# Attention and graph recurrence on one core: the adjacency product in 64x64 tiles, and an earlier start for chunk 0's graph attention

## Chip, core and metric

The kernel runs on one core of a Trainium2 chip. The metric is the device time of one execution in microseconds (us). TensorE (PE) multiplies matrices and transposes into PSUM, VectorE (DVE) and ScalarE (ACT) read PSUM and SBUF, GpSimd (POOL) works on SBUF and issues some DMAs, SyncE (SP) issues the others. They run side by side and meet at semaphores.

## What is computed

x is 128 batches of 64 nodes with 256 features. Four pre-norm residual layers follow each other; in each, `h = relu(layernorm(x))`:

```
x = x + attention_0(h)      # 8 heads, masked by adj, q k v o projections
x = x + attention_1(h)      # 8 heads, and a layernorm of its output added
x = x + graph_attention(h)  # hW; e = leaky(s1 + s2) * adj; softmax; elu(att hW + beta hW)
x = x + recurrence(h)       # 3 steps of:
    a  = adj @ h
    z  = sigmoid(w3(a) + u3(h));  r = sigmoid(w4(a) + u3(h))
    hv = tanh(w5(a) + u5(r * h)); h = (1 - z) * h + z * hv
```

adj (64x64) is symmetric and is the same for every batch, so that `in_mat` and `out_mat` of the recurrence are the same matrix and the two halves of w3, w4 and w5 are added beforehand.

## The kernel before

x stays in SBUF for the whole run as 64 tiles of 128 rows (two batches each), in 16 chunks of four tiles. Weight products are exact to fp32 by splitting both operands into a high and a low fp32r part, three matmuls for one (`product`, L99). PSUM is two tensors of four banks: `scores` (called `high` outside the attention) and `ring`.

**Attention.** `iterations` runs 32 iterations (T = 32, 16 chunks in each of two layers) as a pipeline: in iteration i PE multiplies the scores of chunk i (`scores_piece`), transposes the probabilities of chunk i-1 (`p_transposes`) and the rows of i+1, applies the output weights to i-2 (`o_products`), forms the values of i-1 (`values`), and projects q, k and v of i+1. The last loop body is i = T-2; everything of T-1 and later is written out by hand behind it on each engine, mixed with the graph attention of chunks 0 and 1. Each engine works strictly through its own list, so the order in which these calls are written is the order of the work.

**Graph attention** of one chunk goes: statistics (`rows_stats`, DVE), `norm` (POOL), `graph_normalise` (ACT), `graph_rows` (PE transposes), `graph_high` (ACT) and `graph_low` (DVE), four `graph_product` (PE) with `copy_hw` (ACT), `graph_s2` (PE), `graph_scores` (DVE), `g_shift` (POOL), `g_exponential` (ACT), `graph_attention` (DVE), `graph_attT` (PE), `copy_attT` (DVE), `graph_aggregate` (PE), `graph_out` (ACT and DVE). Then the same sort of norm (`recurrence_stats`, `norm(rn, ..)`, `norm_rows(rn, ..)`) and `enter` (PE, ACT, DVE) bring the chunk into the recurrence.

**Recurrence.** Two chunks run in turn, one step of one chunk is a "half", 48 of them, and a last one that only ends step 3. Six halves are a group of two chunks; from half 1 of each group on, the graph attention of the next two chunks is woven in (`graph_a`: transposes and products, `graph_b`: softmax and aggregation); the last group has none. PE's list in a half: transpose the new h to token rows (`tok`, in steps 2 and 3), u3 product, the adjacency product (L1545: eight matmuls of 128x128 by 128, since adjT is held block-diagonal for two batches), the u5 product of r*h, then w4, w3 and w5 products of the result `agg`. ACT's list: copy tok (L808), two tanh of z (L814), copy the first half of hu (L818), round r*h to its high part (L824, `rhp_hi`), copy the second half of hu (L829), copy agg's high parts (L835), tanh of hv (L839) and so on. DVE makes r*h (L1194), waits for `rhp_hi`, and forms the low part (L1196, `rhp_lo`), for which PE's u5 product waits.

## Time and profile before

| what | value |
|---|---|
| three runs, median (lowest to highest) | 1593.96 us (1591.88 to 1594.06) |
| the profiled execution, device time | 1595.16 us |
| its span in the trace | 1593.1 us |
| what lies around the span | 2.06 us |
| PE busy | 1510.5 us, 95% of the span |
| DVE, ACT, POOL busy | 1243.9, 993.0, 533.7 us |

How to read it: the times of steps below are starts in us from the span's start. The attention ends near 625 us, the recurrence runs from about 640 us to the end. Busy times are of one execution, and the device time is that of the span and 2.06 us around it.

### The profile page before, as it was taken

Reading aid. Unit: us, or ns where it says so; the run is one execution under the profiler, and the core shown is the slowest. Engines: PE = TensorE matmul, PEld = TensorE weight load, DVE = VectorE, ACT = ScalarE, POOL = GpSimd, SP = SyncE. Lnnn points to the kernel's source line nnn. Section 1 sums busy time; section 2 is a strip of 40 time slices with the busy share of each in tenths; the row PEclk is TensorE's granted clock in tenths of the full one; section 3 lists DMA queues with packets and bytes.
Section 4 is the critical chain, followed back from the end, with each engine's and each line's share of the span. In section 5 each row is a group of like instructions: output and inputs, shape, how many; then the busy total and the mean of one; then the engine's idle time right before and its main releaser. Section 6 shows DMA issues by size and latency. Waiting matters only on the chain.

```text
span 1593.1 us, 40455 instructions
## 1 busy us (share of the span) xinstructions
PE 1510.5 (95%) x16248; PEld 1299.4 (82%) x16248; DVE 1243.9 (78%) x2511; ACT 993.0 (62%) x1793; POOL 533.7 (34%) x622
## 2 busy tenths in 40 slices
PE   3899999899999987799999999999999999999997
PEld 3789989798888876588888888888888888888885
DVE  2787887988899986677877877877777777778666
ACT  3676677667777774565666566655665566566553
POOL 1666766667787893300101111111111111111000
PEclk9999999999999998899999999999999999999998
DMA  9200000003322242100000000000000000000000
GB/s 251 82 3 0 0 0 1 15 16 61 61 53 53 56 78 29 27 0 1 27 1 1 27 0 0 26 0 0 26 0 0 26 0 0 27 1 0 27 1 26
DMA packets 36760, 40.12 MB, mean 25 GB/s; under 512 B 11840, under 2 KB 31808, under 8 KB 36672
## 3 DMA queue, kind: packets, MB, share of 16 engines
q0 software_dynamic: 4608, 16.78, 5.6%
q1 hardware_dynamic: 32064, 22.10, 4.8%
q8 instruction: 64, 1.05, 0.3%
q14 instruction: 24, 0.20, 0.0%
HBM read 13.71 MB, written 8.39 MB: 14 GB/s over the span
## 4 chain that ended last, share of the span: by engine, by line
PE 68%; DVE 15%; ACT 7%; issue 5%; POOL 4%; DMA 1%; SPq 0%; DVEq 0%; POOLq 0%; ACTq 0%
PE ring L99 30%; PE scores L99 23%; PE scores L1545 3%; PE ring L1343 2%; PE scores L1307 2%; DVE rhp_lo L1196 2%; PE ring L1490 2%; DVE total L955 2%; POOL s L530 1%; PE ring L1380 1%; ACT rhp_hi L824 1%; ACT later_w L814 1%; PE ring L1508 1%; PE ring L1463 1%; ACT later_w L808 1%
## 5 line engine op out<-in xcount | busy, mean ns | idle before, releaser
L1196 DVE TENSOR_TENSOR rhp_lo<-r,rhp_hi 128x1024 fp32r<-128x1024 f32 x48 | 58.8, 1225 | 157.0 <-ACT rhp_hi L824 157.0
L530 POOL TENSOR_TENSOR s<-s,mx 128x512 f32<-128x512 f32 x128 | 137.9, 1102 | 46.3 <-DVE mx L951 46.3
L536 POOL TENSOR_TENSOR s<-s,rtotal 128x512 f32<-128x512 f32 x128 | 131.4, 1056 | 36.7 <-DVE rtotal L957 36.5
L594 POOL TENSOR_TENSOR r_var_eps<-r_mean_var,eps 128x4 f32<-128x4 f32 x16 | 8.1, 509 | 384.3 <-DVE r_mean_var L1105 384.3
L669 ACT ACTIVATE s<-s 128x512 f32<-128x512 f32 x128 | 78.4, 644 | 76.1 <-POOL s L530 75.9
L839 ACT ACTIVATE hv<-scores,bias 128x512 f32<-128x512 f32 x96 | 66.1, 689 | 83.6 <-PE scores L99 83.6
L946 DVE SCALAR_TENSOR_TENSOR s<-scores,mask 128x512 f32<-128x512 f32 x128 | 87.2, 681 | 32.4 <-PE scores L1307 32.4
L808 ACT ACTIVATE later_w<-ring 128x512 f32<-128x512 f32 x64 | 34.8, 595 | 121.9 <-PE ring L1508 121.9
L681 ACT ACTIVATE pT<-ring 128x512 f32<-128x512 f32 x128 | 66.1, 604 | 47.1 <-PE ring L1343 47.1
L951 DVE TENSOR_REDUCE mx<-s 128x8 f32<-128x512 f32 x128 | 87.9, 686 | 4.4
L857 ACT ACTIVATE r<-r,bias_half 128x512 f32<-128x512 f32 x96 | 64.3, 717 | 37.7 <-DVE r L1221 37.7
L99 PE MATMUL scores<-rhp_hi,u5T_hi 128*128 128x512 f32 x192 | 80.4, 419 | 4.0 <-DVE rhp_lo L1196 1.8
L955 DVE TENSOR_REDUCE total<-s 128x8 f32<-128x512 f32 x128 | 82.6, 645 | 0.0
L1232 DVE TENSOR_TENSOR later_w<-scores,hu 128x512 f32<-128x512 f32 x96 | 64.4, 686 | 19.6 <-PE scores L99 18.8
L99 PE MATMUL ring<-agg_hi,w4T_hi 128*128 128x512 f32 x192 | 78.9, 411 | 0.0
L99 PE MATMUL scores<-agg_hi,w3T_hi 128*128 128x512 f32 x192 | 78.3, 408 | 0.0
L594 POOL TENSOR_TENSOR g_var_eps<-g_mean_var,eps 128x4 f32<-128x4 f32 x16 | 7.3, 457 | 209.5 <-DVE g_mean_var L1105 209.5
L99 PE MATMUL scores<-agg_hi,w5T_hi 128*128 128x512 f32 x192 | 77.0, 401 | 0.0
L99 PE MATMUL ring<-agg_lo,w4T_hi 128*128 128x512 f32 x192 | 76.2, 397 | 0.0
L99 PE MATMUL ring<-agg_hi,w4T_lo 128*128 128x512 f32 x192 | 76.2, 397 | 0.0
L99 PE MATMUL scores<-agg_hi,w5T_lo 128*128 128x512 f32 x192 | 75.9, 395 | 0.0
L99 PE MATMUL scores<-rhp_lo,u5T_hi 128*128 128x512 f32 x192 | 75.8, 395 | 0.0
(295 smaller groups left out, 5251.2 us busy)
## 6 DMA issues: line engine op xcount, KB each, us to landing
x<-beta_less_one POOLq DMA_DIRECT2D x16, 512.0 KB, 4.6
x<-o POOLq DMA_DIRECT2D x16, 512.0 KB, 6.5
out_x<-x SPq DMA_DIRECT2D x16, 512.0 KB, 2.9
x<-in_x SPq DMA_DIRECT2D x1, 6656.0 KB, 30.5
later_w<-in_L_gnn_w_w SPq DMA_DIRECT2D x3, 512.0 KB, 7.2
x<-in_x SPq DMA_DIRECT2D x1, 1024.0 KB, 10.9
stage<-in_L_gnn_w_qkv SPq DMA_DIRECT2D x3, 256.0 KB, 3.0
x<-in_x SPq DMA_DIRECT2D x1, 512.0 KB, 3.5
```

What stands on the lines that cost most here:

```text
L99: last = pe.matmul(out, s, m, start=(begins and n == 0), stop=(ends and n == len(terms) - 1))
L530: pool.tensor_tensor(sr, sr, mx[:, r, :].unsqueeze(2).to_broadcast([P, CT * 2, N]), ALU.subtract).then_inc(s_shifted, 1)
L536: pool.tensor_tensor(sr, sr, rtotal[:, r, :].unsqueeze(2).to_broadcast([P, CT * 2, N]), ALU.mult).then_inc(p_ready, 1)
L669: act.activation(s[:, par, r, :, :, :], s[:, par, r, :, :, :], ACT.Exp).then_inc(p_exp, 1)
L681: act.activation(pT[:, r, :, :].rearrange("p t q -> p (t q)"), ring[:, r, :], ACT.Copy).then_inc(pT_copied, 1)
L839: act.activation(hv[:, m, :], high[:, 2 + m, :], ACT.Tanh, bias=bias[:, 2, m:m + 1])\
L857: act.activation(r[:, m, :], r[:, m, :], ACT.Tanh, bias=bias_half[:, 1, m:m + 1], scale=0.5)\
L946: dve.scalar_tensor_tensor(sr(par, r), scores[:, r, :].rearrange("p (a k) -> p a k", k=N), SCALE, masks[layer_of(i, lay)][:].unsqueeze(1). ...
L951: dve.reduce_max(mx[:, r, :], sr(par, r), AX.X).then_inc(s_max, 1)
L955: dve.reduce_sum(total[:, r, :], sr(par, r), AX.X).then_inc(p_total, 1)
L1196: dve.tensor_tensor(rhp.lo[:], r[:], f32(rhp.hi[:]), ALU.subtract).then_inc(rh_lo_ready, 1)
L1232: dve.tensor_tensor(z[:, m, :], high[:, m, :], hu[:, m, :], ALU.add).then_inc(z_added, 1)
```

## The change

Three things are changed.

1. **Adjacency product.** Instead of eight 128x128 matmuls with a block-diagonal matrix, 32 matmuls of 64x64 by 64: rows 0-63 and 64-127 (g), output partitions 0-63 and 64-127 (c), on four quarters of the array. What belongs to g goes to bank g, so each copy to `agg` writes a strided pattern, and both banks are ready only at the end.
2. **ACT's list in a half.** The rounding of r*h comes ahead of the two tanh of z and the first copy of hu.
3. **The seam between attention and recurrence.** The normalised rows, transposes and products of chunk 0's graph attention move into iteration T-2 (with `g_hT_first` as a buffer of its own), its softmax and output into the work of T-1. Chunk 1's transposed attention, aggregation, output and entry move behind the adjacency product of half 0. POOL's and ACT's output norms of the last attention chunks move too.

Two waits in a half on a loop's count are written with `wait_apart`. The core of the diff (renamed parameters, and DVE's hand-written list in part, are left out):

```diff
+        g_hT_first = Parts(plan, "g_hT_first", [P, FT, CW], start["later_w"] + 4096)
...
-        hw_next = sb("hw_next", [P, CT, WX], F32, start["s"] + 8192)
+        hw_next = sb("hw_next", [P, CT, WX], F32, start["w_ext"])
...
-        h = [sb(f"h_{q}", [P, FT, CW], F32, start["o_n"] + 4096 * n) for n, q in enumerate("ab")]
+        h = [sb("h_a", [P, FT, CW], F32, start["w1o_hi"]), sb("h_b", [P, FT, CW], F32, start["o_n"])]
...
+                norms(T - 1, 1, 1)
+                norm(gn, 1, 1)
                 pool.wait_ge(v_ready, T * 2)
+                pool.memset(att[:], 0.0).then_inc(att_cleared, 1)
                 pool.memset(adjT[:], 0.0).then_inc(adj_cleared, 1)
-                pool.memset(att[:], 0.0).then_inc(att_cleared, 1)
+                shift(T - 1, 1, 0)
+                shift(T - 1, 1, 1)
+                g_shift(0)
+                beta_to_x(T - 1, 1)
+                o_to_x(T - 1, 1, 1)
+                shift(T - 1, 1, 2)
+                shift(T - 1, 1, 3)
+                scale(T - 1, 1, 1)
+                for q in range(R):
+                    normalise(T - 1, 1, q)
+                norm(rn, 0, 0)
...
                 g_shift(1)
-                norm(rn, 0, 0)
                 norms(T + 1, 1, 1)
                 o_to_x(T + 1, 1, 1)
-                scale(T + 1, 1, 1)
-                norm(rn, 1, 1)
...
+                    if isinstance(i, int) and i == T - 2:
+                        graph_normalise(0, 0)
...
+                        if i == T - 2:
+                            graph_high(0, high, 0, g_hT_first)
...
+                        if isinstance(i, int) and i == T - 2:
+                            for t in range(CT):
+                                copy_hw(0, t, high, 2)
...
                     if not s.first:
+                        act.wait_ge(rh_done, n)
+                        if isinstance(n, int) and n == 1:
+                            act.wait_ge(x_plus_o, 16 * CHUNKS)
+                            act.wait_ge(x_plus_beta, 16 * CHUNKS)
+                        act.activation(rhp.hi[:], r[:], ACT.Copy).then_inc(rh_hi_ready, 1)
...
-                    if not s.first:
-                        act.wait_ge(rh_done, n)
-                        if isinstance(n, int) and n == 1:
-                            act.wait_ge(x_plus_o, 16 * CHUNKS)
-                            act.wait_ge(x_plus_beta, 16 * CHUNKS)
-                        act.activation(rhp.hi[:], r[:], ACT.Copy).then_inc(rh_hi_ready, 1)
...
+                        for g in range(2):
+                            act.wait_ge(agg_ready, n * FT + g + 1)
+                            act.activation(agg.hi[:].rearrange("p m (t g q) -> p g m t q", t=CT, g=2)[:, g],
+                                           high[:, g, :].rearrange("p (m t q) -> p m t q", m=FT, t=CT), ACT.Copy)\
+                                .then_inc(agg_hi_ready, 1)
...
+                    if s.first:
+                        o_normalise(T + 1, 1, 1)
...
+                    if s.first:
+                        graph_out(1, high, 2)
+                        norm_rows(rn, r_hn[1], 1, 1)
+                        enter(1, 1)
                     if s.graph_norm is not None:
                         graph_normalise(s.graph_norm, 0 if s.k == 0 else 1)
+                    if s.first:
+                        o_normalise(T + 2, 0, 1)
...
-                act.wait_ge(xT_ready, T * FT)
-                graph_normalise(0, 0)
                 copy_pT(T - 1)
                 o_normalise(T - 1, 1, 1)
-                for q in range(R - 1):
-                    exponential(T - 1, 1, q)
-                graph_high(0, high)
+                exponential(T - 1, 1, 0)
+                exponential(T - 1, 1, 1)
+                g_exponential(0)
+                graph_normalise(1, 1)
                 o_high(T - 2)
-                exponential(T - 1, 1, R - 1)
-                graph_normalise(1, 1)
+                exponential(T - 1, 1, 2)
+                exponential(T - 1, 1, 3)
+                graph_high(1, high, 2)
+                graph_out(0, high, 0)
+                copy_pT(T)
                 for t in range(CT):
-                    copy_hw(0, t, high, 2)
-                copy_pT(T)
-                graph_high(1, high)
+                    copy_hw(1, t, high, 2, hw_next)
+                norm_rows(rn, r_hn[0], 0, 0)
+                o_high(T - 1)
+                g_exponential(1)
+                enter(0, 0, high, 0)
                 o_normalise(T, 0, 1)
-                g_exponential(0)
-                o_high(T - 1)
-                for t in range(CT):
-                    copy_hw(1, t, high, 0, hw_next)
-                graph_out(0, high, 2)
-                g_exponential(1)
-                norm_rows(rn, r_hn[0], 0, 0)
-                graph_out(1, high, 0)
-                enter(0, 0, high)
-                o_normalise(T + 1, 1, 1)
                 act.wait_ge(b_ready, 5)
-                norm_rows(rn, r_hn[1], 1, 1)
...
+                    if isinstance(i, int) and i == T - 2:
+                        graph_low(0, high, 0, g_hT_first)
...
+                    if isinstance(i, int) and i == T - 2:
+                        rows_stats(gn, 1, x_final)
...
+                        for g in range(2):
+                            dve.wait_ge(agg_hi_ready, n * FT + g + 1)
+                            dve.tensor_tensor(agg.lo[:].rearrange("p m (t g q) -> p g m t q", t=CT, g=2)[:, g],
+                                              high[:, g, :].rearrange("p (m t q) -> p m t q", m=FT, t=CT),
+                                              f32(agg.hi[:]).rearrange("p m (t g q) -> p g m t q", t=CT, g=2)[:, g],
                                               ALU.subtract).then_inc(agg_lo_ready, 1)
+                    if s.first:
+                        copy_attT(1, high, 2)
...
+                    if s.first:
+                        graph_out(1, high, 2)
+                        recurrence_stats(1)
...
+                    if s.first:
+                        enter(1, 1)
...
-                sums(T - 1, 1, 0)
-                sums(T - 1, 1, 1)
-                graph_low(0, high)
-                sums(T - 1, 1, 2)
-                sums(T - 1, 1, 3)
+                graph_low(1, high, 2)
                 o_stats(T - 1, 1, 1)
-                final_sum(T - 1, 1, 1)
-                dve.tensor_scalar(beta_ident[:], ident[:], g_beta[:, 0:1], None, ALU.mult).then_inc(beta_ident_ready, 1)
-                graph_scores(0, high, 2)
-                graph_low(1, high)
                 take_first(T, 0, 1)
                 take_out(T - 2, 1, 0, 1)
...
-                graph_attention(1)
-                copy_attT(1, high, 0)
+                enter(0, 0, high, 0)
+                o_stats(T + 1, 1, 1)
                 final_sum(T, 0, 1)
...
+                    if isinstance(i, int) and i == T - 1:
+                        pe.wait_ge(g_hT_lo_ready, FT)
+                        pe.wait_ge(hw_copied, CT)
...
+                    if i == T - 2:
+                        pe.wait_ge(s_masked, (i + 1) * R)
+                        graph_rows(0, high)
...
+                        if isinstance(i, int) and i == T - 2:
+                            pe.wait_ge(g_hT_lo_ready, FT)
+                            pe.wait_ge(gw_lo_ready, 2)
+                            for t in range(CT):
+                                wait(pe, hw_copied, t - 1)
+                                graph_product(0, t, high, 2, g_hT_first)
...
-                            pe.wait_ge(tok_copied, (s.later - 1) * 2)
+                            wait_apart(pe, tok_copied, (s.later - 1) * 2)
...
-                            pe.wait_ge(z_added, n * FT)
+                            wait_apart(pe, z_added, n * FT)
...
-                            pe.wait_ge(x_plus_pos, 4)
...
                         rows = r_hn[s.me] if s.step == 0 else tok
-                        for m in range(FT):
-                            for t in range(CT):
-                                last = pe.matmul(high[:, m, t * P:(t + 1) * P], rows[:, t, m * P:(m + 1) * P],
-                                                 adjT[:], start=True, stop=True)
-                            last.then_inc(agg_ready, 1)
+                        for t in range(CT):
+                            for m in range(FT):
+                                for g in range(2):
+                                    own = slice(g * N, (g + 1) * N)
+                                    for c in range(2):
+                                        f = m * P + c * N
+                                        last = pe.matmul(
+                                            high[c * N:(c + 1) * N, g, (m * CT + t) * N:(m * CT + t + 1) * N],
+                                            rows[own, t, f:f + N], adjT[own, own], start=True, stop=True)
+                                    if t == CT - 1 and m == FT - 1:
+                                        last.then_inc(agg_ready, 1)
...
+                    if s.first:
+                        graph_attT(1, high, 2)
...
+                    if s.first:
+                        graph_aggregate(1, high, 2, hw_next)
...
+                        if s.first:
+                            pe.wait_ge(x_plus_pos, 4)
...
+                    if s.first:
+                        pe.wait_ge(hu_copied, FT)
+                        enter(1, 1)
...
                 scores_piece(T - 1)
                 p_transposes(T - 1, 1)
+                pe.wait_ge(s_masked, (T - 1) * R + 1)
+                graph_s2(0, high, 0, g_hT_first)
                 o_products(T - 1, 1)
-                pe.wait_ge(s_masked, (T - 1) * R + 2)
-                graph_rows(0, high)
                 values(T - 1, 1)
-                pe.wait_ge(g_hT_lo_ready, FT)
-                pe.wait_ge(gw_lo_ready, 2)
+                graph_attT(0, high, 0)
                 pe.wait_ge(s_masked, T * R)
-                for t in range(CT):
-                    wait(pe, hw_copied, t - 1)
-                    graph_product(0, t, high, 2)
-                graph_s2(0, high, 2)
+                graph_rows(1, high, 2)
+                graph_aggregate(0, high, 0)
                 p_transposes(T, 0)
-                graph_rows(1, high)
-                o_products(T, 1)
-                values(T, 0)
-                graph_attT(0, high, 2)
                 pe.wait_ge(g_hT_lo_ready, 2 * FT)
                 for t in range(CT):
                     if t >= 2:
                         pe.wait_ge(hw_copied, CT + t - 1)
-                    graph_product(1, t, high, 0)
-                graph_s2(1, high, 0)
-                graph_aggregate(0, high, 2)
+                    graph_product(1, t, high, 2)
+                o_products(T, 1)
+                graph_s2(1, high, 2)
+                values(T, 0)
                 o_products(T + 1, 1)
-                graph_attT(1, high, 0)
-                graph_aggregate(1, high, 0, hw_next)
                 pe.wait_ge(x_plus_pos, 2)
-                enter(0, 0, high)
+                enter(0, 0, high, 0)
                 halves(pe, half)
```

**PE, first loop group of the recurrence, half 1.** `hp` is h in its two parts, `g_hn` the normalised rows of the next chunk, `rhp` is r*h. Before:

```order
L99 MATMUL ring<-hp_b_lo,u3T_hi 128x512
L99 MATMUL ring<-hp_b_hi,u3T_lo 128x512
L1463 MATMUL ring<-ident,g_hn 128x128 x8
L1545 MATMUL scores<-adjT,r_hn_b 128x128 x8
L99 MATMUL scores<-rhp_hi,u5T_hi 128x512
L99 MATMUL scores<-rhp_lo,u5T_hi 128x512
```

and now:

```order
L99 MATMUL ring<-hp_b_lo,u3T_hi 128x512
L99 MATMUL ring<-hp_b_hi,u3T_lo 128x512
L1508 MATMUL ring<-ident,g_hn 128x128 x8
L1593 MATMUL scores<-adjT,r_hn_b 64x64 x32
L99 MATMUL scores<-rhp_hi,u5T_hi 128x512
L99 MATMUL scores<-rhp_lo,u5T_hi 128x512
```

Only the adjacency product has another form; its neighbours are the same.

**ACT, half 2 of the first group** (`later_w` is tok in the first row and z in the next, `e` the graph softmax). Before:

```order
L808 ACTIVATE later_w<-ring 128x512 x2
L814 ACTIVATE later_w<-later_w,bias_half 128x512 x2
L818 ACTIVATE hu<-ring 128x512
L824 ACTIVATE rhp_hi<-r 128x1024
L786 ACTIVATE e<-e 128x256
L829 ACTIVATE hu<-ring 128x512
L835 ACTIVATE agg_hi<-scores 128x512 x2
```

and now:

```order
L829 ACTIVATE later_w<-ring 128x512 x2
L837 ACTIVATE rhp_hi<-r 128x1024
L841 ACTIVATE later_w<-later_w,bias_half 128x512 x2
L845 ACTIVATE hu<-ring 128x512
L807 ACTIVATE e<-e 128x256
L850 ACTIVATE hu<-ring 128x512
L856 ACTIVATE agg_hi<-scores 128x8x64 x2
```

The rounding of r*h has moved up by three instructions, and the rest keeps its order.

**ACT, entry of the recurrence, half 0.** `o_n` is the norm of an attention output, `r_hn_b` and `hp_b` belong to chunk 1. Before:

```order
L692 ACTIVATE o_n<-o,shift_by,rstd 128x256 x4
L768 ACTIVATE r_hn_b<-x,r_shift_by,r_rstd 128x256 x4
L692 ACTIVATE o_n<-o,shift_by,rstd 128x256 x4
L818 ACTIVATE hu<-ring 128x512
L829 ACTIVATE hu<-ring 128x512
L835 ACTIVATE agg_hi<-scores 128x512 x2
L800 ACTIVATE hp_b_hi<-ring 128x512
```

and now:

```order
L706 ACTIVATE o_n<-o,shift_by,rstd 128x256 x4
L845 ACTIVATE hu<-ring 128x512
L850 ACTIVATE hu<-ring 128x512
L856 ACTIVATE agg_hi<-scores 128x8x64 x2
L706 ACTIVATE o_n<-o,shift_by,rstd 128x256 x4
L882 ACTIVATE r<-r,bias_half 128x512 x2
L813 ACTIVATE later_w<-scores 128x512 x2
L816 ACTIVATE later_w<-later_w 128x1024
L789 ACTIVATE r_hn_b<-x,r_shift_by,r_rstd 128x256 x4
L821 ACTIVATE hp_b_hi<-ring 128x512
```

The copies of hu and agg, for which PE waits in half 0, now stand ahead of the last output norms and of chunk 1's normalised rows; chunk 1's graph output has moved in between.

## Rows read from the trace of the kernel before

**Rows 1.** The page: span, and busy time of each engine

```profile
span 1593.1 us, 40455 instructions
PE 1510.5 (95%) x16248; PEld 1299.4 (82%) x16248; DVE 1243.9 (78%) x2511; ACT 993.0 (62%) x1793; POOL 533.7 (34%) x622
```

**Rows 2.** Busy time by stretch: us, busy (x), granted TensorE clock, DMA share, GB/s

```profile
700.00:1500.00 800.00, 795.07 (x4201) 667.06 (x4201) 623.65 (x1112) 490.72 (x855) 83.52 (x117) 1.00 0.03 10
```

**Rows 3.** Groups of instructions on PE over the execution: the adjacency product

```profile
L1545 PE MATMUL scores<-adjT,later_w 128*128 128x128 f32 x512 | 62.3, 275 | 0.0
...
L1545 PE MATMUL scores<-adjT,r_hn_b 128*128 128x128 f32 x128 | 15.6, 275 | 0.0
```

**Rows 4.** PE in order of time around one adjacency product: start, us, what

```profile
906.32 1.95 PE L1545 MATMUL scores<-adjT,r_hn_b 128*128 128x128 f32 x16
908.03 0.48 PE L99 MATMUL scores<-rhp_hi,u5T_hi 128*128 128x512 f32 x1
908.35 0.40 PE L99 MATMUL scores<-rhp_lo,u5T_hi 128*128 128x512 f32 x1
```

**Rows 5.** PE in order of time around one `values`, in tiles of 64x32

```profile
502.77 0.28 PE L99 MATMUL ring<-w1o_hi,oT_lo 128*128 128x256 f32 x1
502.98 1.49 PE L1380 MATMUL ring<-pT,v 64*32 64x64 f32 x128
504.39 0.50 PE L99 MATMUL ring<-hT_hi,w1q_hi 128*128 128x512 f32 x1
504.73 0.39 PE L99 MATMUL ring<-hT_lo,w1q_hi 128*128 128x512 f32 x1
```

**Rows 6.** The same `values` alone in short stretches; (x) counts records in flight

```profile
503.03:503.11 0.08, 0.08 (x16) 0.08 (x24) 1.00 0.00 0
503.11:503.17 0.06, 0.06 (x24) 0.06 (x25) 1.00 0.00 0
```

**Rows 7.** ACT, DVE and PE in order of time, one half of the last group

```profile
1542.72 1.09 ACT L808 ACTIVATE later_w<-ring 128x512 f32<-128x512 f32 x2 [3.27 <-PE ring L1508]
1543.69 1.33 ACT L814 ACTIVATE later_w<-later_w,bias_half 128x512 f32<-128x512 f32 x2
...
1545.40 1.06 ACT L824 ACTIVATE rhp_hi<-r 128x1024 fp32r<-128x1024 f32 x1
...
1547.71 0.60 ACT L835 ACTIVATE agg_hi<-scores 128x512 fp32r<-128x512 f32 x1 [0.28 <-PE scores L1545]
...
1541.00 1.22 DVE L1194 SCALAR_TENSOR_TENSOR r<-r,h_b 128x1024 f32<-128x1024 f32 x1
1546.49 1.23 DVE L1196 TENSOR_TENSOR rhp_lo<-r,rhp_hi 128x1024 fp32r<-128x1024 f32 x1 [4.28 <-ACT rhp_hi L824]
1547.64 1.40 DVE L1204 TENSOR_TENSOR agg_lo<-scores,agg_hi 128x512 fp32r<-128x512 f32 x2
...
1547.78 0.50 PE L99 MATMUL scores<-rhp_hi,u5T_hi 128*128 128x512 f32 x1
```

**Rows 8.** Who waited for whom on PE, 583.6 to 700 us: total, times, longest

```profile
PE ring L1463 <- ACT hu L829: 9.2, 1, 9.2
PE scores L1482 <- DVE att L1143: 6.6, 2, 4.8
PE scores L99 <- DVE g_hT_lo L1114: 5.9, 1, 5.9
PE ring L99 <- DVE hp_a_lo L1168: 3.2, 1, 3.2
```

**Rows 9.** Busy time by stretch, the seam from v's projection to half 1

```profile
583.60:670.20 86.60, 60.21 (x690) 52.86 (x690) 57.87 (x138) 47.70 (x93) 39.34 (x54) 0.84 0.25 38
```

**Rows 10.** The chain that ended last, in the seam: start, us, what

```profile
645.16 2.81 POOL o_n L560
...
650.28 1.57 ACT r_hn_b L768 x3
651.85 1.96 ACT o_n L692 x4
```

108 lines of the change are left out of this document (55 added, 53 removed).

## Prediction

> **What bounds the kernel now.** First the page and the table of stretches: PE is busy 95% of the span [rows 1] and 795 of 800 us between 700 and 1500, at the full clock [rows 2]. So in the recurrence the time is the sum of what PE has to do; DVE (78%) and ACT (61%) wait for it there. Next the groups of instructions on PE. The adjacency product comes in 768 records (512, and twice 128, since chunks a and b have a row each, of which one is shown [rows 3]), which at 16 records a product [rows 4] is 48 products. Then the waits of PE and the table of stretches at the seam: between 583.6 and 670.2 us PE is busy for only 60.2 of 86.6 us, at a mean granted clock of 0.84 [rows 9], and four waits hold most of the idle time [rows 8]. These are the two places where the change can gain: less work in 48 halves, and a seam with fewer holes.
>
> **Part 1, the adjacency product.** Before: from its start at 906.32 to the second matmul behind it at 908.35 are 2.03 us, of which 0.23 are the first u5 matmul's own pace (as between any two of 512 columns); so it costs 1.80 us [rows 4]. Its quarter form is not in this trace, but `values` is close: 64x32 tiles, 64 columns, the same fp32, 128 records. From the last full-array matmul before it at 502.77 to the second one behind at 504.73 are 1.96 us; less the two neighbours' own pace (0.23 for 512 columns and half of it for 256) that is 1.61 us for 128 records on eight tiles, 16 on each, with the entering and leaving of the tiled form included [rows 5]. The new product has 64 records on four tiles, again 16 on each. Two readings of `values` give two prices. (a) If a tile's own turn is the limit, 16 records cost the same 1.61 us: 0.19 us saved. (b) If eight tiles together are limited by how fast records are issued, four tiles are limited by their streams. The short stretches speak for (b): near the start of `values` eight more records begin in about 0.06 us [rows 6], and those are both records of four matmuls on four tiles, which means that a tile finishes its two records in about 0.11 us. This is also what half of 128 columns costs at 0.11 us a record [rows 4]. Then the new product takes 16 x 0.056 = 0.90 us. What `values` spends on entering and leaving I take as 0.3 us (1.61 less 128 records at some 10 ns each). Sum 1.2 us, 0.57 us saved by the unrounded starts. I take (b), since its rows show a tile keep that pace; 0.19 is the bound on one side, and 0.65 (no more than 0.25 for entering and leaving) on the other. 47 halves outside the seam: 27 us, bounds 9 and 31.
>
> The full-array neighbours have to drain around a tiled product: behind `values` the first two matmuls start 0.34 us apart [rows 5], behind the adjacency product before, 0.32 us [rows 4]; most of the 0.3 us lies before the first of them. The Trainium skill (TensorEngine Tiling (Array Packing), Key Properties) says that changing the tiling mode drains TensorE, which speaks against this change, as it adds two changes of mode to every half; the trace agrees that they cost something, and by the rows they are already in the sum.
>
> **Part 2, r*h first on ACT.** A gain on PE counts only if the u5 product, next in PE's list, isn't then waiting for `rhp_lo`. In the last group it is already close: `rhp_lo` starts at 1546.49, takes 1.23, and u5 starts at 1547.78, right behind it [rows 7]. Without part 2 nothing of part 1 would be left in such a half. r*h itself is ready at 1542.2 (1541.00 + 1.22), and tok is copied by 1543.8; now rounding begins there rather than at 1545.40, so `rhp_lo` ends 1.6 us earlier, near 1546.1, where PE wants it at 1547.2. Spare: 1.1 us. The tanh of z and hu are 1.0 us later, behind which `agg_hi` is queued on ACT; that list ends when it ended before, because its sum hasn't changed, and ACT still had to wait 0.28 us for the product then [rows 7]. With the product 0.57 us earlier that cover is gone by 0.3 us, which the spare of the next step takes up. Both banks of agg are now ready only at the end of the product, so the two copies (0.60 each, overlapping slightly) and the two DVE subtractions (1.40) end some 2.0 us behind it rather than 1.3 [rows 7]; the u5 product of 12 x 0.23 = 2.8 us covers that, and the spare falls to 0.8 us. Strided writes of 64 in a row I cost at nothing. So nothing but PE stays the bound, and all of part 1 counts. The small waits for `rhp_lo` that go are worth 0 to 2 us; I take 0.
>
> **Part 3, the seam.** It moves PE's work (for chunk 0's graph attention eight transposes and 24 products of 258 columns, some 0.12 us each, 3.9 us) into iteration T-2, where PE has no hole; this neither gains nor costs by itself. What goes: the 5.9 us wait for `g_hT_lo` of chunk 0, the 6.6 us for the two softmaxes, 9.2 us for hu, and 3.2 us for `hp_a_lo` [rows 8], in all 25 of the 26.4 us idle [rows 9]. The 9.2 us are the last link of a chain of output norm, POOL's scale (2.81), normalised rows of chunk 1 and another output norm, all ahead of hu on ACT [rows 10]; with the new list hu needs none of them. What comes instead, from walking the five lists through the new order with the durations of this trace, as estimates: 1.1 us for chunk 0's softmax, 5.5 us before the last `p_transposes`, because `graph_out(0)` stands between the `sums` on DVE and the exponential on ACT is behind it, so that POOL's `normalise` is late; 3.4 us for chunk 1's `g_hT_lo`, which stands behind `recurrence_stats(0)`; 1.8 us for `oT_lo`; 2 us for `hp_a_lo`; 1.7 us for `agg_lo` in half 0; then 3.7 and 2.1 us for chunk 1's entry, which waits for its graph output, statistics, norm and rows in turn. With small ones 21.5 us, against 26.4: 5 us less idle. The lower clock cost about 0.16 of 60.2 = 9.6 us [rows 9]; the new holes are shorter but as many, and I give it half of that, 5 us less. So the seam gains 10 us; the bounds are 1 us (POOL or DVE later than I walked, the same clock) and 15 us (full clock throughout).
>
> **The sum.** Profiled execution 1595.2 - 27 - 10 = 1558 us; the median of the three runs lies 1.2 us below that execution. I forecast 1557.5 us; its own range is 1549 to 1567.
>
> **Rivals.**
> 1. *Reading (a)*: a tile's turn is the limit. For it: away from its start `values` falls behind the pace of rows 6, to 1.49 us in all [rows 5]. Then 9 us, and 1595 - 1 - 9 - 10 = 1575 us.
> 2. *The seam is given back*: DVE's list in T-1 is long, and one late step (`graph_out` between the sums) moves all behind it. For it: five engines meet there. Against: the longest wait is plainly taken out of ACT's list. Then 1594 - 27 = 1567 us.
> 3. *Slower: the four tiles don't run at the same time*, since two share a bank and two share rows. 64 records at 0.056 is 3.6 us and with 0.3 that is 3.9 us against 1.80: 47 x 2.1 = 99 us, 1594 + 99 - 10 = 1683 us. It decides for a loss from about 27 ns a record on (64 x 27 ns + 0.3 = 2.0 us, a product 0.2 us dearer, which eats the seam's 10 us). Against: `values` makes a record every 12 ns [rows 5] with tiles that share banks and rows as well.
> 4. *A floor for each matmul*: if a small record couldn't start more often than every 25 ns, 64 records would take 1.6 us and with 0.3 that is 1.9: 5 us lost, 10 gained, 1589 us. Such a floor of about 25 ns is stated by the Trainium skill (TensorE: Matmul & The Clock Gate, Wait — 56ns, not 53.3ns?). 128 records in 1.49 us [rows 5] contradict it for tiled records, so it has little weight.
>
> **How the numbers follow.** Forecast 0.63; rival 1 0.19; rival 2 0.10; rival 4 0.02; rival 3 0.04; no change within 0.2%, by gains that new waits in the halves eat, 0.02. The range 1549 to 1578 takes in rivals 1 and 2. Within 0.2% (3.2 us) is about what a measurement of this kernel can tell from no change. Faster 0.94, same 0.02, slower 0.04.
>
> **What would show it.** The adjacency product as 64 records in 0.9 to 1.2 us on PE (right), 1.5 or more (rival 1), over 3 (rival 3). A group of two chunks (six halves) should take 3.4 us less, with PE still over 98% busy between 700 and 1450; if PE waits for `rhp_lo` or `agg_lo` there, part 2 is wrong. DVE's wait for `rhp_hi` should fall by 1.6 us a half. The second adjacency product should start near 660 us instead of at the end of the stretch of rows 9, and no single PE wait in the seam should be over 6 us. The forecast fails if the tiled product costs more than 1.6 us, or if the second adjacency product starts later than 669 us.

## The result and the profile after

| kernel | median (lowest to highest) | profiled execution |
|---|---|---|
| before, beside these runs | 1593.95 us (1591.88 to 1594.06) | 1595.2 us |
| the change | 1581.98 us (1579.63 to 1582.67) | 1582.7 us |

The ratio is 0.9925, with a 95% interval of 0.9908 to 0.9943: 12 us faster, where 36 were forecast, and outside the range. The two profiled executions differ by 12.5 us (their spans by 12.4), and the trace says where they lie. Marks for this are the starts of the scores product of chunks T-2 and T-1 (128 records `scores<-kT,qT` each) and of the adjacency products:

| from, to | before | after | change | forecast |
|---|---|---|---|---|
| start to scores of T-2 | 566.2 | 568.4 | +2.2 | 0 |
| to scores of T-1 | 17.4 | 22.8 | +5.4 | +3.9 |
| to the 2nd adjacency product | 86.6 | 85.8 | -0.8 | -13.9 |
| to the 48th adjacency product | 892.6 | 873.3 | -19.3 | -27 |
| to the end | 30.4 | 30.5 | +0.1 | 0 |

The page of the changed kernel, span and busy time of each engine; it answers to [rows 1]:

```profile
span 1580.7 us, 45104 instructions
PE 1488.1 (94%) x18552; PEld 1263.8 (80%) x18552; DVE 1245.9 (79%) x2511; ACT 994.1 (63%) x1793; POOL 534.4 (34%) x622
```

PE has 22.4 us less work, but the span is only 12.4 us shorter: 10 us of it has become idle time. The table of stretches, 700 to 1500 us, answers to [rows 2]:

```profile
700.00:1500.00 800.00, 787.52 (x6247) 646.23 (x6248) 639.02 (x1136) 499.55 (x870) 83.78 (x117) 1.00 0.03 10
```

PE's idle time there was 4.9 us and is 12.5. The product itself: one of its three groups of instructions answers to [rows 3], and PE in order of time (start, us, what) to [rows 4]:

```profile
L1593 PE MATMUL scores<-adjT,later_w 64*64 64x64 f32 x2048 | 37.2, 221 | 0.0
```

```profile
908.82 1.04 PE L1508 MATMUL ring<-ident,g_hn 128*128 128x128 f32 x8
909.79 1.16 PE L1593 MATMUL scores<-adjT,r_hn_b 64*64 64x64 f32 x64
...
911.21 0.40 PE L99 MATMUL scores<-rhp_lo,u5T_hi 128*128 128x512 f32 x1
```

64 records, and 1.42 us from its start to the second u5 matmul where it was 2.03. ACT and DVE in one half of the last group, changed kernel, answer to [rows 7]:

```profile
1531.00 1.09 ACT L829 ACTIVATE later_w<-ring 128x512 f32<-128x512 f32 x2 [3.28 <-PE ring L1553]
1531.97 1.06 ACT L837 ACTIVATE rhp_hi<-r 128x1024 fp32r<-128x1024 f32 x1
```

```profile
1533.06 1.23 DVE L1223 TENSOR_TENSOR rhp_lo<-r,rhp_hi 128x1024 fp32r<-128x1024 f32 x1 [2.58 <-ACT rhp_hi L837]
1535.92 1.29 DVE L1231 TENSOR_TENSOR agg_lo<-scores,agg_hi 128x512 fp32r<-128x512 f32 x2 [1.63 <-ACT agg_hi L856]
```

The rounding follows the copy of tok at once, and DVE's wait for it is 2.58 us instead of 4.28; over the whole execution 70.7 us instead of 157.0, 1.8 us a half (forecast 1.6). Who waited for whom on PE in two stretches of the changed kernel (total, times, longest): 700 to 1480 us, and 583.6 to 700 us, which answers to [rows 8]:

```profile
PE ring L1646 <- DVE hp_a_lo L1195: 6.0, 7, 0.9
PE ring L1646 <- DVE hp_b_lo L1195: 4.7, 6, 0.9
PE ring L99 <- issue: 1.7, 4, 0.8
PE scores L99 <- DVE rhp_lo L1223: 1.1, 1, 1.1
```

```profile
PE ring L1379 <- DVE oT_lo L996: 7.6, 1, 7.6
PE ring L99 <- DVE hp_a_lo L1195: 6.2, 1, 6.2
PE ring L99 <- DVE oT_lo L996: 4.6, 1, 4.6
PE ring L1508 <- ACT r_hn_b L789: 3.6, 1, 3.6
PE scores L1527 <- DVE att L1170: 2.4, 1, 2.4
PE ring L99 <- DVE hp_b_lo L1195: 2.0, 1, 2.0
PE ring L99 <- DVE agg_lo L1231: 1.5, 1, 1.5
PE scores L99 <- DVE g_hT_first_lo L1141: 1.4, 1, 1.4
```

Of the four old waits of [rows 8] the one for hu is gone, and those for the softmax (6.6 to 2.4 us) and for chunk 0's `g_hT_lo` (5.9 to 1.4, now `g_hT_first_lo`) are smaller. The one for `hp_a_lo` has grown from 3.2 to 6.2 us, and one of 7.6 us for `oT_lo` is new. The table of stretches from T-1's scores to the second adjacency product answers to [rows 9]:

```profile
591.20:677.00 85.80, 57.86 (x707) 49.75 (x706) 52.76 (x124) 42.74 (x81) 35.37 (x48) 0.78 0.26 39
```

Idle 27.9 us of 85.8, where it was 26.4, at a granted clock of 0.78 instead of 0.84. The chain that ended last, in the seam of the changed kernel, answers to [rows 10]:

```profile
609.61 1.23 DVE x L1190
...
612.46 1.27 DVE r_stats L1127 x4
614.15 0.57 DVE o L989
614.72 0.61 DVE oT_lo L996
615.37 3.68 PE ring L1379 x16
...
640.45 1.95 ACT o_n L706 x4
642.47 1.29 DVE o L989 x2
643.76 1.21 DVE hp_a_lo L1195 x2
645.01 5.49 PE ring L99 x12
```

The old chain through POOL's scale and two output norms ahead of hu is gone, as forecast. The new one goes through DVE's list twice.

### The profile page after: what moved, and what is told of

Read it like the earlier page. It is cut to its first block, busy times and chain, and to the rows that moved or that the text cites. A ratio compares the mean times of both kernels' runs of the same rounds, so it can differ in the third digit from the quotient of the medians.

```text
span 1580.7 us, 45104 instructions
## 1 busy us (share of the span) xinstructions
PE 1488.1 (94%) x18552; PEld 1263.8 (80%) x18552; DVE 1245.9 (79%) x2511; ACT 994.1 (63%) x1793; POOL 534.4 (34%) x622
## 4 chain that ended last, share of the span: by engine, by line
PE 72%; DVE 15%; ACT 5%; issue 4%; POOL 2%; DMA 1%; SPq 0%; DVEq 0%; POOLq 0%; ACTq 0%
PE ring L99 35%; PE scores L99 21%; PE ring L1379 3%; PE scores L1593 3%; PE scores L1340 2%; PE ring L1416 2%; PE ring L1535 2%; PE ring L1553 2%; DVE hv L1211 1%; DVE r L1252 1%; DVE total L978 1%; DVE hv L1209 1%; PE ring L1646 1%; PE ring L1390 1%; POOL s L531 1%
## 5 line engine op out<-in xcount | busy, mean ns | idle before, releaser
L1223 DVE TENSOR_TENSOR rhp_lo<-r,rhp_hi 128x1024 fp32r<-128x1024 f32 x48 | 60.2, 1254 | 70.7 <-ACT rhp_hi L837 70.7
L1231 DVE TENSOR_TENSOR agg_lo<-scores,agg_hi 128x512 fp32r<-128x512 f32 x96 | 61.7, 685 | 45.1 <-ACT agg_hi L856 44.7
L99 PE MATMUL scores<-rhp_hi,u5T_lo 128*128 128x512 f32 x192 | 76.4, 398 | 0.0
L99 PE MATMUL scores<-agg_lo,w5T_hi 128*128 128x512 f32 x192 | 75.8, 395 | 0.0
```

What stands on the lines that cost most here:

```text
L99: last = pe.matmul(out, s, m, start=(begins and n == 0), stop=(ends and n == len(terms) - 1))
L1223: dve.tensor_tensor(rhp.lo[:], r[:], f32(rhp.hi[:]), ALU.subtract).then_inc(rh_lo_ready, 1)
L1231: dve.tensor_tensor(agg.lo[:].rearrange("p m (t g q) -> p g m t q", t=CT, g=2)[:, g], high[:, g, :].rearrange("p (m t q) -> p m t q", m=FT ...
```

## Experiments

The theory after this reading has four parts. In the halves, (1) the tiled product saves its 0.5 us only where PE is the bound, (2) the early rounding of r*h is a gain of its own, (3) halves in which a chunk enters and one leaves are bound by DVE, and the jump at the end of a loop round has become visible; and (4) the new seam is slower than the old because of two places in the hand-written lists. The rival for all of it is that the halves took what was forecast and the seam, or a lower clock, lost more.

### The halves and the seam apart

Three kernels, made of the kernel before and one or two parts of the change. The edits, cut to their core:

```diff
# tiles alone: on PE the loop of 32 small matmuls as in the change, on ACT and DVE the copies to agg by g
-                        for m in range(FT):
-                            for t in range(CT):
-                                last = pe.matmul(high[:, m, t * P:(t + 1) * P], rows[:, t, m * P:(m + 1) * P],
+                        for t in range(CT):
+                            for m in range(FT):
+                                for g in range(2):
# tiles and the early rounding: the same, and on ACT, ahead of the two tanh of z
                     if not s.first:
+                        act.wait_ge(rh_done, n)
+                        act.activation(rhp.hi[:], r[:], ACT.Copy).then_inc(rh_hi_ready, 1)
# the seam alone: the changed kernel with both of these turned back
```

All three have the change's two `wait_apart` on PE.

> The kernel before with the adjacency product in quarter tiles and r*h first on ACT, and the old seam. Theory: the halves alone gave 19 us of the changed kernel's gain and its seam lost 5 to 7 us, so this one takes about 1594 - 19 = 1575 us, faster than the changed kernel (1582). Rival: the halves gained less by themselves and the two parts help each other (a chunk that enters earlier removes waits later); then about 1580 us or more.

> The kernel before with the adjacency product in quarter tiles only; r*h keeps its old place on ACT. Theory: the u5 product then waits for rhp_lo in the halves with transposed tokens, whose old spare was nearly nothing, so most of the gain is missing: 1594 - 5 = 1589 us (range 1585 to 1592), with PE waits for rhp_lo of 0.4 to 0.6 us in some 40 halves. Rival: PE had spare there and the move on ACT adds nothing; then the same time as with both parts, about 1575 us.

> The changed kernel with the old adjacency product (eight 128x128 matmuls) and the old place of r*h, so that only the seam is new. Theory: the seam costs what the trace shows up to the second adjacency product, 4.6 us and perhaps the 2 us of lower clock in the attention: 1598 to 1601 us. Rival: the seam is neutral or gains (1584 to 1594 us) and the halves lost something to it.

Measured against the kernel before: tiles and rounding 1572.6 us, ratio 0.9869 (0.9837 to 0.9902), 21 us faster; tiles alone 1588.8 us, 0.9967 (0.9946 to 0.9988), 5 us faster; the seam alone 1600.6 us, 1.0039 (1.0024 to 1.0054), 6 us slower. So the halves brought less than 27 us and the seam cost 6: the rival, that the halves took all that was forecast, falls. PE's waits from 700 us to the end, tiles alone:

```profile
PE scores L99 <- DVE rhp_lo L1198: 24.1, 33, 1.8
...
PE ring L99 <- issue: 2.6, 4, 0.8
```

PE now waits for `rhp_lo` 33 times. In 19 of the 46 distances between the products (the table below: 2 to 3 and 4 to 5 in seven groups, and the last five) that leaves nothing of the product's gain. That is the prediction's "Without part 2 nothing of part 1 would be left in such a half".

The seam and the two parts of the halves don't add up quite: 21 less 6 is 15 us, where the change gave 12. In the traces its halves are 1.6 us longer than those of tiles and rounding (873.3 against 871.7 us), since the new seam reaches into their first group (20.76 and 20.77 us for 20.33 and 19.20). The rest is no more than executions differ by in their attention stages (last section).

### The early rounding alone

> The kernel before, with nothing changed but the place of the rounding of r*h: first on ACT, ahead of the two tanh of z and the first copy of hu. Theory A, that of the prediction: the old product hid the rounding, so that PE gains 0 to 2 us from the earlier rounding by itself, 1592 to 1594 us against about 1594 to 1596 of the kernel before, and the distances of the adjacency products in a group stay 20.84 and 20.06 us. Theory B: the rounding was already the limit by 0.3 us in the halves at 20.06 and 19.18 us and in the last group (the tiles with the earlier rounding took 0.86 us from each of these, and only 0.51 from the halves at 20.84 us); then 14 halves in the loop and 5 in the last group fall by 0.35 us, 6 to 7 us in all, 1587 to 1588 us, and the 20.06 becomes 19.7 us.

Measured: 1587.1 us, ratio 0.9949 (0.9933 to 0.9965): 8 us faster, which is theory B (the same edit, by the prediction, was worth 0 to 2 us). Between the second and the last adjacency product it is 886.6 us against 892.6, 6.0 us; the rest lies before it, in the attention and the seam, where executions differ by as much. The edit is the one `rhp.hi` line above, in the kernel before. The step that was missed stands in the trace of before, but in no list of waits. PE and DVE in order of time around the product of the half behind that of [rows 4], kernel before:

```profile
927.16 1.95 PE L1545 MATMUL scores<-adjT,later_w 128*128 128x128 f32 x16
929.22 0.50 PE L99 MATMUL scores<-rhp_hi,u5T_hi 128*128 128x512 f32 x1
```

```profile
927.94 1.23 DVE L1196 TENSOR_TENSOR rhp_lo<-r,rhp_hi 128x1024 fp32r<-128x1024 f32 x1 [3.63 <-ACT rhp_hi L824]
```

In [rows 4] u5 starts 1.71 us after the product's start; here it starts 2.06 us after it, right behind `rhp_lo` (927.94 + 1.23 = 929.17). These 0.35 us are not listed as a wait, since the last small matmuls' ends are modelled until 929.11. With the early rounding, the same place:

```profile
922.60 1.95 PE L1545 MATMUL scores<-adjT,later_w 128*128 128x128 f32 x16
924.31 0.48 PE L99 MATMUL scores<-rhp_hi,u5T_hi 128*128 128x512 f32 x1
```

1.71 us again. Seventeen halves (two in each of seven groups, three in the last) were late by this, 17 x 0.35 = 6.0 us.

The distances from one adjacency product to the next put the parts side by side, in us, for one group of the loop and (last three rows) around and in the last group:

| half | before | rounding alone | tiles alone | tiles and rounding | the change |
|---|---|---|---|---|---|
| 1 to 2 | 20.84 | 20.84 | 20.33 | 20.33 | 20.33 |
| 2 to 3 | 20.06 | 19.70 | 20.07 | 19.20 | 19.20 |
| 3 to 4 | 20.84 | 20.84 | 20.33 | 20.33 | 20.33 |
| 4 to 5 | 19.18 | 18.83 | 19.20 | 18.32 | 18.32 |
| 5 to 6 | 18.13 | 18.14 | 18.05 | 18.04 | 18.03 |
| 6 to 1 | 19.00 | 19.00 | 18.9 to 20.0 | 18.9 to 19.8 | 18.9 to 19.9 |
| 6 to 1, into the last group | 17.53 | 17.53 | 17.54 | 17.03 | 17.04 |
| last group, 1 to 2 | 16.63 | 16.63 | 16.60 | 16.13 | 16.13 |
| last group, its last three | 17.0 | 16.65 | 17.0 | 16.15 | 16.15 |

With both, the product is worth 0.5 us in four of a group's six halves and in the last group, the rounding 0.36 more in two of the six and in the last three; in the halves 5 to 6 and 6 to 1 of a group there is no such gain. In the halves 2 to 3 and 4 to 5, 14 in all, and in the last three, the tiles alone give 0 and the rounding alone 0.36, but both 0.87, since two limits lie side by side there; in the two in front of those three each alone gives 0 and both 0.5. This is how two parts that bring 5 and 8 us alone bring 21 together.

### The halves with an entering and a leaving chunk

DVE in order of time of the changed kernel, behind the adjacency product that starts at 987.96:

```profile
989.79 1.29 DVE L1231 TENSOR_TENSOR agg_lo<-scores,agg_hi 128x512 fp32r<-128x512 f32 x2 [1.56 <-ACT agg_hi L856]
990.99 1.40 DVE L1127 BATCH_NORM_STATS2 r_stats<-x 128x6 f32 x4
...
996.83 1.28 DVE L1252 TENSOR_TENSOR r<-ring,hu 128x512 f32<-128x512 f32 x2
998.03 1.27 DVE L1195 TENSOR_TENSOR hp_a_lo<-ring,hp_a_hi 128x512 fp32r<-128x512 f32 x2
```

The same subtraction in the kernel before:

```profile
989.11 1.43 DVE L1204 TENSOR_TENSOR agg_lo<-scores,agg_hi 128x512 fp32r<-128x512 f32 x2
```

From 989.79 to 999.30 DVE doesn't stop, and at its end stands the low part of the entering chunk, for which PE waits 0.9 us before the transposes of the leaving one. `agg_lo` ends 3.1 us behind the product's start, where it was 3.3 in the same half of before (987.25 to 990.54): both banks come at the end of the shorter product, and `agg_lo` now waits 1.56 us for the copies, so DVE's list starts 0.2 us earlier and not 0.5. If DVE's list is what holds PE up here, the low part of the entering chunk needs only to be made earlier:

```diff
+                    if s.enters is not None and not s.first:
+                        enter(s.enters, s.other)
                     if not s.last:
                         dve.wait_ge(hu_copied, (n + 1) * FT)
...
-                    if s.enters is not None and not s.first:
-                        enter(s.enters, s.other)
```

> The changed kernel with DVE's low part of the entering chunk ahead of the additions of r in each half with an entry. Theory: in the two halves of a group with an entry and a leaving chunk DVE is last: its agg copies end only 0.2 us earlier than before the change, and PE waits 0.8 to 0.9 us for hp_lo before it transposes the leaving chunk, 10.7 us in 13 waits. With 1.3 us less ahead of hp_lo these waits go: 1582 - 10 = 1572 us (1570 to 1575). Rival: the additions of r, 1.3 us later, hold up something else (r's tanh, r*h, the u5 product), and the time changes by less than 3 us.

Measured: 1568.0 us, ratio 0.9816 (0.979 to 0.9842), 14 us better than the change by the medians and 13.3 us between the 2nd and the 48th product (860.0 against 873.3), more than the 10 us that the edit was meant to save. The distances 5 to 6 and 6 to 1 are 16.99 and 17.9 to 18.9 us. PE's waits, 700 to 1480 us, are only these:

```profile
PE ring L99 <- issue: 1.7, 4, 0.7
PE scores L99 <- DVE rhp_lo L1223: 1.1, 1, 1.1
```

It gives 1 us a half, where the tiles had 0.5 to gain. So the kernel before should have been losing the other 0.5 already. Its own list of PE's waits (700 to 1480 us), which the prediction didn't take up, shows this for six of the 13 halves; the edit was not tried in the kernel before.

```profile
PE ring L1592 <- DVE hp_b_lo L1168: 2.3, 6, 0.5
```

The jump of the loop on PE: in the change the distance 6 to 1 differs from round to round, 18.96, 19.42, 19.92, 19.49, 19.47, 18.91 us, with PE's waits put down to "issue"; with the old product and the new seam (the seam alone, which has the `wait_apart` too) it is 18.98 to 19.06 in all, and with the tiles and the old seam it spreads as in the change. So the spread comes with the 64 records. With the halves written out on PE, in place of the loop:

```diff
-                halves(pe, half)
+                for k in range(HALVES + 1):
+                    half(Half(0, k))
+                for g in range(1, GROUPS):
+                    for k in range(1, HALVES + 1):
+                        half(Half(g, k))
```

> The changed kernel with PE's halves of the loop groups written out instead of in a loop; the other engines keep their loops. Theory: the first half of each loop round comes 0 to 1 us late (18.9 to 19.9 us from the adjacency product before it, where it was 19.0 each time before the change), with PE waiting for nothing the profile shows, because its longer loop body has to be fetched again at the jump. Without the jump the distance is 18.9 us in all groups and the time 3 us less, 1579 us. Rival: the loop doesn't matter and the spread stays; the same time within 1 us, or slower by more fetching.

Measured: 1576.2 us, ratio 0.9878 (0.9855 to 0.9901); between the 2nd and the 48th product 871.0 us against 873.3, the distance is 18.95 or 18.96 in every round, and "issue" is gone from the waits. That 2.3 us go this way is shown; the rest of the 6 us of the medians is no more than executions differ by outside the halves (last section).

### The seam

Two waits were to be taken away. `enter(0)` makes PE wait for `hp_a_lo`; on DVE this stands behind `take_first(T + 1)`, which overwrites the o that ACT's `o_normalise(T)` still reads, and that stands on ACT behind `enter(0)`'s own copies. DVE's waits, 583.6 to 700 us, the change:

```profile
DVE o L989 <- ACT o_n L706: 8.4, 1, 8.4
```

First edit, on ACT (fix_norm); second, on DVE with the first (fix_both):

```diff
+                o_normalise(T, 0, 1)
                 o_high(T - 1)
                 g_exponential(1)
                 enter(0, 0, high, 0)
-                o_normalise(T, 0, 1)
...
+                take_out(T - 3, 1, 1, 1)
+                o_low(T - 2)
                 sums(T - 1, 1, 1)
-                graph_out(0, high, 0)
                 sums(T - 1, 1, 2)
                 sums(T - 1, 1, 3)
-                recurrence_stats(0)
-                take_out(T - 3, 1, 1, 1)
-                o_low(T - 2)
                 graph_low(1, high, 2)
+                graph_out(0, high, 0)
+                recurrence_stats(0)
```

> The changed kernel with one call moved on ACT: the output norm of chunk T-3 (o_normalise(T)) ahead of chunk 0's entry into the recurrence instead of behind it. Theory: DVE's take_first(T+1) waited 8.4 us for it and chunk 0's low part stood behind that, for which PE waited 6.2 us; that wait goes down to about 1 us, and the time by 5 us: 1577 us. Rival: the wait is taken over by the norm's own inputs (POOL's shift, DVE's statistics), and the time stays within 1 us of 1582.

> fix_norm, and on DVE the last output take_out(T-3) and o_low(T-2) moved ahead of the sums, and graph_out(0) and recurrence_stats(0) behind the sums and graph_low(1). Theory: PE's 7.6 us wait for oT_lo before the last p_transposes comes from DVE's list alone; it falls to 3 us or less (then POOL's normalise is last) and the time from 1572.8 to 1568 us (1566 to 1571). Rival: what is gained there is lost at chunk 0's entry, since its statistics come later; then 1572 to 1574 us.

Measured: the first 1572.8 us, ratio 0.9862 (0.9833 to 0.989); both 1571.2 us, 0.9842 (0.9823 to 0.9862). By the medians the first is worth 9 us, and the second nothing that can be told. The wait for `hp_a_lo` went from 6.2 to 2.4 us, where about 1 was expected. With the second edit that of 7.6 us for `oT_lo` is gone, and 2.3 us for POOL's `normalise` stand in its place, as expected; the expected 5 us of the median don't show. The profiled execution of the second took 1577.6 us, the other three 1571.1 to 1571.2, and its scores of T-2 start at 572.5 us, 5.3 us later than in that of the first. The clearer measure is inside the trace. From the scores of T-2 to the second adjacency product, which leaves out the attention before and the halves, the kernels take:

| kernels | us |
|---|---|
| old seam (before, rounding alone, tiles alone, tiles and rounding, and the old seam with mended halves) | 104.0, 101.9, 102.3, 104.8, 103.7 |
| new seam (seam alone, the change, its two forms with other halves) | 109.4, 108.5, 107.5, 107.1 |
| new seam, output norm moved (fix_norm and best_new) | 103.3, 104.7 |
| new seam, DVE's list changed too (fix_both and all_fixes) | 99.7, 96.7 |

On the average the first edit takes 4 us from the seam and the second 6, but executions of one and the same seam differ by 1 to 3 us. The stretch from T-1's scores to the second adjacency product says what repeats and what doesn't. Here it is with the first edit and with both (fix_norm, all_fixes):

```profile
590.06:670.50 80.44, 55.88 (x705) 48.61 (x704) 54.20 (x124) 43.69 (x83) 35.67 (x48) 0.83 0.27 41
```

```profile
590.88:664.70 73.82, 54.41 (x705) 46.29 (x704) 53.97 (x124) 43.89 (x83) 35.68 (x48) 0.86 0.30 45
```

PE's idle time and the granted clock in this stretch, for the same kernels in the same order:

| kernels | idle, us | granted clock |
|---|---|---|
| old seam | 26.4, 25.8, 26.5, 26.6, 26.1 | 0.84, 0.84, 0.82, 0.80, 0.82 |
| new seam | 27.5, 27.9, 28.9, 29.0 | 0.78, 0.78, 0.82, 0.86 |
| output norm moved | 24.6, 24.8 | 0.83, 0.81 |
| DVE's list changed too | 19.6, 19.4 | 0.82, 0.86 |

The idle time repeats: the first edit takes 3.6 us of it (the wait for `hp_a_lo` fell by 3.8) and the second 5.2 (that before the last `p_transposes` fell by 5.2). The clock doesn't: the same new seam was granted 0.78 in one execution and 0.86 in another, with no less idle time, so that what an edit does to the clock can't be read from one trace each.

### The mended kernels

Halves as in the edits above (the early low part, PE written out), with the old seam, with the new seam and its output norm moved, and with DVE's list changed too:

> The old seam, the tiled adjacency product and the early rounding of r*h, and two edits of mine: DVE makes the entering chunk's low part before it adds the recurrent term to r, and PE's halves are written out in place of a loop. Theory A, that the two losses found in the halves are independent of each other and of the seam: 1572.6 us (tiles and rounding alone) less 2.05 us in each of 7 groups for the entering chunk, 14 us, less 3 to 5 us for the jumps: 1554 to 1556 us, with the six distances of a group at 20.33, 19.20, 20.33, 18.32, 17.0 and 17.9 us in every group. Theory B, that DVE or ACT becomes the limit once PE no longer waits there: distances above these and 1560 us or more.

> The changed kernel with three edits of mine: the last output norm of chunk T ahead of the entry's copies on ACT, DVE's low part of the entering chunk before the additions to r, and PE's halves written out in place of a loop. Theory A, the edits add: 1572.8 us (the output norm's edit alone) less 14 less 3 to 5 us, 1554 to 1556 us, level with the kernel that has the same halves and the old seam, which would say that the new seam, mended in this one place, is worth nothing. Theory B, the new seam mended is worth the 5 us of idle time that it was forecast to take away: 1549 to 1551 us.

> As the kernel with the three edits, and with DVE's hand-written list in iteration T-1 changed too: the sums of the last attention output and the low part of its transposed form come before chunk 0's graph output and its statistics. Theory A, that the wait so removed is taken up by the next one in POOL's scale: 1554 to 1556 us, within 2 us of the kernel without this edit. Theory B, that the clock and the idle time recover with it: 1550 us or less.

Measured: 1555.3 us, ratio 0.9737 (0.9711 to 0.9763); 1559.1 us, 0.9768 (0.974 to 0.9796); 1550.9 us, 0.9711 (0.9686 to 0.9737). The first is as expected, the second 3 us above its expectation, though the spans of the two traces are alike (1556.2 and 1556.3 us). The distances of a group are 20.33, 19.20, 20.33, 18.32, 17.0 and 17.9 in all three, as the halves' theory A has it; only the first group of the new seam still has one of 20.77 in place of 19.20. The new seam with only its output norm moved is worth nothing beside the old; with both edits the profiled seam is 7 us shorter (96.7 against 103.7), and the median 4 us lower, whose interval overlaps that of the old seam. The last of the three is faster than both kernels, 46 us less than before. That its extra edit would be taken up by the next wait is not borne out: POOL's `normalise` takes 2.4 of the 7.6 us, and the other 5.2 come back.

## Why the prediction was wrong, point by point

Two steps failed. In the seam, forecast at -10 us and measured at +4.6, the walk through the lists put PE's wait for `hp_a_lo` at 2 us and the one before the last `p_transposes` at 5.5, and took 5 us for a better clock; the trace has 6.2 and 7.6 us, and no run shows the clock giving anything back. In the halves, "47 halves" of 0.57 us each assumed that only PE is the bound; the gain came in 33 of them, at 0.51 us, and 6.0 us of Part 2, which the prediction put at nothing, hid part of the loss.

**What bounds the kernel.** "In the recurrence the time is the sum of what PE has to do" was read from 795 of 800 us busy [rows 2]. It was true to within 5 us there, and no proof for a faster PE: in 17 halves DVE's `rhp_lo` set the start of u5, and in 13 DVE's list was as late as PE's, in six of them later by up to 0.5 us. A busy share of 99% says what the bound is, not how far the next one lies behind it.

**Part 1, the price.** Right in reading: (b), four tiles side by side, first to last record 0.94 us, or 0.059 us for each of a tile's 16 records (forecast 0.90 and 0.056). From its start to the second u5 matmul less 0.23 it is 1.19 us, the forecast 1.2. But the way in costs 0.1 us in front of its first record (eight transposes ahead of it to its start take 0.97 us, 0.87 before), so a half gains 0.51 us and not 0.57. Rivals 1, 3 and 4 fall: 1.61, 3.9 and 1.9 us aren't there. The floor of 25 ns of the Trainium skill (TensorE: Matmul & The Clock Gate, Wait — 56ns, not 53.3ns?) doesn't hold for tiled records here: 64 start within 0.94 us, 15 ns apart.

**Part 1, the count.** This step failed: "47 halves", and "nothing but PE stays the bound, and all of part 1 counts". 33 distances fell by 0.51, 16.8 us. In the 13 between half 5 and half 1 of the next group DVE is the bound, and the prediction walked only a half of the last group [rows 7], which has no entering chunk. It had seen that both banks are ready only at the end, but asked only whether u5 covers the copies for PE's next product; `agg_lo` is also the head of DVE's list. A row for it stood in the trace of before: PE's wait for `hp_b_lo`, six times, 0.5 us at most.

**Part 2.** "The small waits for `rhp_lo` that go are worth 0 to 2 us; I take 0": they were worth 6.0 us between the products (rounding alone). The claim that part 1 needs part 2 was right, and holds more widely than was said.

**The jump.** It isn't in the prediction, and cost 2.3 us.

So the halves: -16.8 - 6.0 - 0.7 (half 5 to 6) + 2.1 (half 6 to 1, the jump in it) = -21.4 us, and +2.0 in the first group, where the new seam's tail reaches (20.76 and 20.77 us instead of 20.33 and 19.20): -19.4, measured -19.3.

**Part 3.** Forecast -10, measured +4.6 (and 6 by the median of the seam alone). The moved work cost 5.4 us in T-2, 3.9 of work as forecast and 1.4 for `g_hT_first_lo`, a wait that wasn't walked. The idle time was walked at 21.5 us and is 27.9. The walk found the right places: chunk 1's entry 3.7 and 2.1 (3.6 and 2.0 measured), `agg_lo` 1.7 (1.5), softmax 1.1 (2.4), before the last `p_transposes` 5.5 (7.6), `oT_lo` 1.8 (4.6). The 3.4 us for chunk 1's `g_hT_lo` aren't in the list of waits at all. It failed most at `hp_a_lo`, 2 us walked and 6.2 measured: the walk took each call behind its inputs, but not the buffer o that `take_first` may overwrite only when ACT's output norm has read it; with that norm moved ahead the wait is 2.4 us, near the walked one. The wait before `p_transposes` was given to POOL's `normalise`; the trace has `oT_lo` there, which stands behind `graph_out`, the sums and the statistics in DVE's list; the edit that moved all three closed it, so that `graph_out` alone isn't shown to be the cause. The clock, given 5 us back, took 1.6 more in this execution (57.9 us for work of 56.3 at the old clock, [rows 9] less 3.9). Over the executions above it was 0.78 to 0.86 in the new seam and 0.80 to 0.84 in the old: no run shows the 5 us, and what sets it here stays open. By the prediction's own sign (the second adjacency product not later than 669 us; it started at 677.0, 2.2 us of that from the attention) this step failed. So did the sign that no single wait of PE in the seam should be over 6 us. Rival 2 had the mechanism, DVE's list in T-1, at a chance of 0.10, though not its loss.

**The sum**: +2.2 (attention), +4.6 (seam), -19.3 (halves), +0.1 (end): -12.4 us of the profiled spans, where -37 was written.

## To carry to other kernels

When the engine that is busy for 99% is made faster, the time falls by what the second engine leaves free, half by half: before the gain is multiplied by a count, compare the start distances of all kinds of iterations, and take for each the operand that came last (a start right behind a producer's end is a wait, though no list has it). In a hand-written order, walk the buffers that an instruction overwrites as well as those it reads; one reader late on another engine made 3.8 us of a wait of 6.2 here. And a change whose parts seem to belong together is worth timing in parts: here two gave 21 us and the third took 6 back.

## What the runs showed of the hardware

- **The way into tiled form** costs 0.1 us before the first small record on top of what lies behind the start; 64 records of 64x64 by 64 on four tiles take 0.94 us from first to last start, 15 ns each. A strided copy of 64 in a row cost ACT what a plain one did. ACT's groups of instructions for agg's high parts, before and after (count, busy us, mean ns):

```profile
L835 ACT ACTIVATE agg_hi<-scores 128x512 fp32r<-128x512 f32 x96 | 57.3, 602 | 12.2 <-PE scores L1545 12.2
```

```profile
L856 ACT ACTIVATE agg_hi<-scores 128x512 fp32r<-128x512 f32 x96 | 52.4, 602 | 7.3 <-PE scores L1593 7.0
```
- **A loop's jump on PE** left no spread with 16 records in the product (18.98 to 19.06 us in all rounds), and cost 0 to 1 us with 64, differing from round to round, against the loop written out (18.96). The queue of instructions on the two pages (packets, MB, share of 16 engines), before and after:

```profile
q8 instruction: 64, 1.05, 0.3%
```

```profile
q8 instruction: 109, 1.79, 0.5%
```

  PE's instructions went from 16248 to 18552; with the loop written out the queue had 102 packets. That the fetch of instructions is what is late was not tried.
- **The granted clock in the attention** isn't the same in two executions of the same code. The scores of T-2 started between 564.8 and 572.5 us in the thirteen profiled kernels, whose attention is the same up to there. The table of stretches, 300 to 400 us, in the change and in the new seam with mended halves (best_new):

```profile
300.00:400.00 100.00, 95.73 (x1948) 87.23 (x1947) 87.63 (x207) 69.55 (x135) 69.83 (x78) 0.98 0.19 39
```

```profile
300.00:400.00 100.00, 94.50 (x1944) 85.93 (x1943) 88.83 (x208) 69.48 (x135) 70.66 (x78) 1.00 0.20 40
```

  In the second the clock was at its upper level throughout; in the first the mean of 0.98 is what some 4 us at the lower level give. T-2's scores started at 568.4 and 564.8 us. Kernels with the change's attention lie on both sides of the kernel before with its 566.2 us (564.8 and 564.9 in two, 572.5 in one), so the 2.2 us of the first row of the table above aren't shown to be the change's doing. Differences of 2 or 3 us between kernels are therefore read from distances between like products and from idle time here, and from medians only with their interval.
